# A two-layer recurrent block on one core: tiles by channel from memory, B's rows and the second layer's tokens turned through DRAM instead of on TensorE

## The reference

```
xn = layernorm(x)
# layer 0: RWKV-6 time mix (4 heads of 64) and a gated FFN with 2-of-4 sparsity
xx  = previous token of xn - xn
a   = tanh((xn + xx*maa_x) @ w1)            # five rank-32 mixes
x_f = xn + xx*(maa_f + a_f @ w2_f)          # f in w, k, v, r, g
y   = wkv6(r, k, v, w, u); out = groupnorm(y)*silu(g) @ W_o.T
ffn = sparsify_2to4(silu(xn@w_gate)*(xn@w_up)) @ w_down
# layer 1: state space layer (8 heads, state 64, head 64) and a gated FFN
inp, res = split(xn @ w_in.T); dt, B, C = split(xn @ w_param.T)
a   = exp(-softplus(dt))                    # decay of each head and token
S_t = a_t*S_(t-1) + B_t x_t^T ; y_t = C_t S_t
out = (y*silu(res)) @ w_out.T
```

## Time and profile before

| | |
|---|---|
| median of three runs | 761.48 us |
| the profiled execution | 761.46 us |
| its span | 759.7 us |
| busy: PE, DVE, ACT, POOL | 733.9, 505.5, 326.0, 76.6 us |

### The profile page before, as it was taken

How to read it: one execution, slowest core, us unless ns; L and a number is a source line. 1 busy time by engine, 2 the same in 40 slices (tenths; PEclk the granted TensorE clock), 3 DMA queues, 4 the chain that set the end, 5 groups by cost and what they waited for, 6 DMA issues and landing times.

```text
span 759.7 us, 18508 instructions
## 1 busy us (share of the span) xinstructions
PE 733.9 (97%) x7316; PEld 601.5 (79%) x7316; DVE 505.5 (67%) x1177; ACT 326.0 (43%) x659; POOL 76.6 (10%) x85
## 2 busy tenths in 40 slices
PE   5897999999999999999999999999999999999997
PEld 3775778877888788886888868888788878888686
DVE  3886578736797367955778467884679736796143
ACT  1322575226632466214752157512664236631570
POOL 6201011101011011000110001100011101101020
PEclk9999999999999999999999999999999999999999
DMA  8800410005000150002400032001500014000320
GB/s 284 330 16 0 127 30 3 1 30 154 2 3 1 48 135 2 3 2 71 113 2 2 3 126 57 3 1 30 149 8 2 1 45 140 2 3 1 99 55 16
DMA packets 33938, 39.77 MB, mean 52 GB/s; under 512 B 20352, under 2 KB 27968, under 8 KB 32192
## 3 DMA queue, kind: packets, MB, share of 16 engines
q1 hardware_dynamic: 33856, 38.49, 16.9%
HBM read 32.12 MB, written 6.36 MB: 51 GB/s over the span
## 4 chain that ended last, share of the span: by engine, by line
PE 93%; DVE 4%; issue 1%; ACT 1%; DMA 0%; POOL 0%; DVEq 0%; SPq 0%; ACTq 0%; POOLq 0%
PE psum L1276 70%; PE psum L1378 4%; PE psum L1488 2%; PE psum L1473 2%; PE psum L1338 2%; PE psum L1349 1%; PE psum L1499 1%; PE psum L1707 1%; PE psum L1526 1%; PE psum L1304 1%; PE psum L1324 1%; PE psum L1361 1%; PE psum L1434 1%; PE psum L1634 1%; PE psum L1441 1%
## 5 line engine op out<-in xcount | busy, mean ns | idle before, releaser
L519 ACT ACTIVATE BC<-psum 64x256 f32<-64x256 f32 x128 | 81.2, 634 | 3.5 <-PE psum L1276 1.8
L1276 PE MATMUL psum<-xnT,sb_f_gate 128*128 128x256 f32 x248 | 62.6, 396 | 1.0 <-ACT xnT L532 0.8
L1276 PE MATMUL psum<-xn1T,sb_n_gate 128*128 128x256 f32 x256 | 61.4, 383 | 0.0
L1276 PE MATMUL psum<-xn1T,sb_n_up 128*128 128x256 f32 x256 | 60.5, 379 | 0.0
L1276 PE MATMUL psum<-xnT,sb_f_up 128*128 128x256 f32 x240 | 58.3, 385 | 0.0
L1276 PEld LDWEIGHTS psum<-xnT,sb_f_gate 128*128 128x128 f32 x248 | 46.2, 194 | 9.9 <-issue 1.7
L1276 PEld LDWEIGHTS psum<-xn1T,sb_n_up 128*128 128x128 f32 x256 | 48.6, 190 | 6.6
L1276 PEld LDWEIGHTS psum<-xn1T,sb_n_gate 128*128 128x128 f32 x256 | 47.3, 190 | 6.5
L867 DVE TENSOR_TENSOR kT<-kT,dec 128x256 f32<-128x256 f32 x56 | 25.7, 458 | 36.0 <-PE psum L1378 29.0
L1276 PE MATMUL psum<-sb_n_down,hidB 128*128 128x256 f32 x224 | 49.5, 379 | 0.0
L1276 PE MATMUL psum<-sb_f_down,hid 128*128 128x256 f32 x224 | 49.5, 379 | 0.0
(11 more groups left out here) (209 smaller groups left out, 1517.1 us busy)
## 6 DMA issues: line engine op xcount, KB each, us to landing
cs_row<-cs_dram SPq DMA_DIRECT2D x8, 1024.0 KB, 5.5
x_dram<-gate SPq DMA_DIRECT2D x8, 512.0 KB, 2.8
cs_half<-cs_dram SPq DMA_DIRECT2D x16, 256.0 KB, 6.4
hidB<-x_dram SPq DMA_DIRECT2D x8, 512.0 KB, 8.1
X<-in_x SPq DMA_DIRECT2D x9, 256.0 KB, 2.7
x<-in_x SPq DMA_DIRECT2D x8, 256.0 KB, 4.1
out_tokens<-thFB SPq DMA_DIRECT2D x8, 256.0 KB, 2.2
sb_w_rkvgo<-in_w_rkvgo SPq DMA_DIRECT2D x1, 1280.0 KB, 5.9
```

What stands on the lines that cost most here:

```text
L519: ins = a_.activation(cols[:, par, 2 * pair:2 * pair + 2, :], src[64 * par:64 * par + 64, :, s, :], ACT.Identity)
L1276: ins = t_.matmul(ps(t, name)[first_row:first_row + rows, col:col + n], w, x, start=(k == 0), stop=(k == len(ws) - 1))
```

## The change

- x is given to the program a second time, by channel (`x_turned`). The next tile is loaded in both orders. Only the statistics come from the token order; mean and rstd go out to `row_dram` and come back on every partition (`token_rows`), and `next_normed` makes `xnT` directly. `next_turned` and its ScalarE copy are gone.
- B is turned in 32x32 blocks by two DVE instructions of 128x512 (`B_by_block`), stored in four transfers in pieces of 32 elements, and loaded as `Brow`; `B_decayed` scales `Brow` in place. `turned_B` is gone.
- The sums by position are read straight into `cs_pos`, one element at a time, instead of `cs16`; `turned_sums` is gone. `cs_row` has a semaphore of its own.
- The second layer's normed tokens are turned in 32x32 blocks on DVE, stored in eight transfers and loaded as `xn1T` (`channels_1`). Only the first tile is still turned by TensorE, now at the end of the first round.
- The first gate pair of the next tile is computed at the end of a round (`next_gate_0`, `next_up_0`) instead of at the head of the next.
- On DVE `end_args` and `B_by_block` go between level steps; the four counting operations of the sparsity go behind the level steps; the order of the decayed scores is 0, 2, hidden block 3, 1, 3. On ScalarE `end_exp` and `L_exps(0)` come before the tanh of res, `L_exps(1)` before `sums_exp`.
- The last combined round is written out instead of being in the loop.

```diff
-         ["xT1", "csum", "C1", "bt0", "sc1", "ys1", "n1u", "n3u"],
-         ["dt", "B0", "res0", "bt1", "sc3", "n0g", "n2g", "s1"],
+         ["csum", "C1", "sc1", "ys1", "n1u", "n3u"],
+         ["dt", "B0", "res0", "sc3", "n0g", "n2g", "s1"],
...
-            with eng.Fori(1, NT) as it:
+            with eng.Fori(1, NT - 1) as it:
                 one(Tile(it), Tile(it, -1))
+            one(Tile(None, NT - 1), Tile(None, NT - 2))
...
+            def token_rows(a):
+                wait(rstd_ready, a.count(3, 2))
+                wait(rows_loaded, a.count(16, 16))
+                sp_.dma_start(A["row_dram"].rearrange("(q p two) -> p q two", q=NQ, p=P),
+                              token_stats[:, :, :]).then_inc(rows_stored, 16)
+                wait(rows_stored, a.count(16, 16))
+                sp_.dma_start(rows[:, :, :].rearrange("p t two -> p (t two)"),
+                              A["row_dram"].partition_broadcast(P)).then_inc(rows_loaded, 16)
+
+            def channels_1(a, b):
+                wait(xn1_blocks, a.count(1, 0))
+                to = A["n_dram"].rearrange("(c j q g i) -> g q j c i", j=32, q=NQ, g=4, i=32)
+                blocks = xn1_turned[:, :].rearrange("p (c q i) -> p c q i", q=NQ, i=32)
+                for g_ in range(4):
+                    for q in range(NQ):
+                        sp_.dma_start(to[g_, q], blocks[32 * g_:32 * g_ + 32, :, q, :]).then_inc(xn1_stored, 16)
+                wait_filled(sp_, b, "n3u")
+                wait(xn1_stored, a.count(128, 16))
+                sp_.dma_start(xn1T[:, :, :], A["n_dram"].rearrange("(h p t) -> p h t", p=P, t=T)).then_inc(xn1_loaded, 16)
...
+                    sp_.dma_start(XT[:, :, :], channels(a.at() if last else a.next().at())).then_inc(xT_loaded, 16)
...
-                    sp_.dma_start(cs16[:, :], cs_dram.rearrange("(c p) -> c p", p=P)).then_inc(cs_loaded, 16)
-                    sp_.dma_start(flat(cs_row), cs_dram.partition_broadcast(P)).then_inc(cs_loaded, 16)
+                    sp_.dma_start(flat(cs_row), cs_dram.partition_broadcast(P)).then_inc(cs_rows_loaded, 16)
+                    sp_.dma_start(cs_pos[:, :], cs_dram.rearrange("(c p) -> p c", p=P),
+                                  allow_slow_non_contiguous=True).then_inc(cs_loaded, 16)
...
                     sp_.dma_start(Xrow.rearrange("p q c d -> p (q c) d"),
                                   x_dram.rearrange("(c p d) -> p c d", p=P, d=SD)).then_inc(X_rows, 16)
+                    if a:
+                        token_rows(a)
+                    wait(B_rows, b.count(16, 16))
+                    wait(B_blocks, b.count(2, 2))
+                    to = b_dram.rearrange("(s n i e d) -> s e i n d", s=NQ, i=32, e=2, d=32)
+                    for s in range(NQ):
+                        for e in range(2):
+                            r = 64 * s + 32 * e
+                            sp_.dma_start(to[s, e], B_turned[r:r + 32, :].rearrange("p (n d) -> p n d", d=32)).then_inc(
+                                B_stored, 16)
+                    wait(B_stored, b.count(64, 64))
+                    sp_.dma_start(Brow.rearrange("p q c d -> p (q c) d"),
+                                  b_dram.rearrange("(c p d) -> p c d", p=P, d=SD)).then_inc(B_rows, 16)
+                    if a:
+                        channels_1(a, b)
...
                 def next_normed():
-                    norm_apply(X, xn, a.count(3, 2), xn_ready)
-
-                    d.tensor_scalar(xnT[:, :, 0:1], xnT[:, :, T:T + 1], keep[:, bass.ds(a.next().at(), 1)], None,
-                                    ALU.mult).then_inc(carry_ready, 1)
+                    dve.wait_ge(rows_loaded, a.count(16, 32))
+                    dve.wait_ge(xT_loaded, a.count(16, 16))
+                    did(d.tensor_tensor(XT[:, :, :], XT[:, :, :], rows[:, :, 0].unsqueeze(1).to_broadcast([P, CH, T]),
+                                        ALU.subtract))
+                    did(d.tensor_scalar(xnT[:, :, 0:1], xnT[:, :, T:T + 1], keep[:, bass.ds(a.next().at(), 1)], None,
+                                        ALU.mult))
+                    after()
+                    d.tensor_tensor(xnT[:, :, 1:T + 1], XT[:, :, :], rows[:, :, 1].unsqueeze(1).to_broadcast([P, CH, T]),
+                                    ALU.mult).then_inc(xn_ready, 1)
...
+                    if b:
+                        dve.wait_ge(xn1_ready, a.count(1, 1))
+                        d.transpose(xn1_turned[:, :], flat(habs[:, 0:2, :])).then_inc(xn1_blocks, 1)
...
+                def B_by_block(half):
+                    wait_freed(dve, b, "B0")
+                    wait_freed(dve, b, "B1")
+                    n = slice(half * SEQ_T * SH // 2, (half + 1) * SEQ_T * SH // 2)
+                    d.transpose(B_turned[:, n], BC[:, 0, :, :].rearrange("p t h -> p (t h)")[:, n]).then_inc(B_blocks, 1)
...
                     level_step(a, 2)
+                    end_args()
+                    B_by_block(0)
+                    level_step(a, 3)
+                    B_by_block(1)
+                    level_step(a, 4)
                     sparse_compare(a, 0, 1)
                     sparse_compare(a, 0, 2)
-                    level_step(a, 3)
-                    sparse_sums()
-                    level_step(a, 4)
-                    sparse_rest()
                     level_step(a, 5)
...
-                        wait_freed(pe, b, "xT1")
+                        pe.wait_ge(xn1_loaded, b.count(16, 16))
...
-                    for s in range(NQ):
-                        wait_freed(pe, b, f"bt{s}")
+                    pe.wait_ge(B_ready, b.count(1, 1))
...
                 if a and b:
-                    gates_0()
-                    turned_1()
                     rank_mix()
...
-                    turned_sums()
-                    turned_B()
                     scores(0)
...
                     ffn_n(b, 3)
-                    next_turned()
                     out_1()
                     ffn_1(b, hidB)
+                    if a.reg is not None:
+                        next_gate_0()
+                        next_up_0()
```

More of the change, by code:

```diff
@@ L122, in build_block @@
         W = {n: sb("sb_" + n, list(A[n].shape)) for n in A
-             if n not in ("x", "out", "cs_dram", "x_dram", "w_mix2b", "w_dec2")}
+             if n not in ("x", "out", "x_turned", "n_dram", "row_dram", "cs_dram", "b_dram", "x_dram", "w_mix2b", "w_dec2")}
         W["w_mix2b"], W["w_dec2"] = sb("sb_mix2b", [NQ * DMIX, C]), sb("sb_dec2", [NQ * DDEC, C])
@@ L140, in build_block @@
         xn = sb("xn", [P, NQ, C])
+        XT = sb("XT", [P, CH, T])
+        token_stats = sb("token_stats", [P, NQ, 2])
+        rows = sb("rows", [P, T, 2])
         xnT = sb("xnT", [P, CH, T + 1])
@@ L187, in build_block @@
         cs_nat = sb("cs_nat", [P, NQ, SH])
-        cs16 = sb("cs16", [NQ * SCH, P])
+        cs_pos = sb("cs_pos", [P, NQ * SCH])
         cs_col = sb("cs_col", [P, NQ * SCH])
@@ L392, in one @@
                         out_stored, 16)
[L395 removed]
+            for s in (X_rows, X_stored, cs_stored, cs_loaded, cs_rows_loaded, B_rows, out_stored, rows_loaded, xn1_stored):
                 sp_.sem_inc(s, 16)
@@ L410, in _ @@
             load(["n_gate", "n_up", "n_down"], "ffn1")
+            token_rows(Tile(None, 0, first=True))
             with sp_.Fori(1, NT - 1) as it:
@@ L637, in out_scaled @@
                     free(ins, a, "yT")
-                def next_copied():
-                    act.wait_ge(carry_ready, a.count(1, 1))
-                    xnT_copy(a.next())
                 def ffn_tanh_1():
@@ L649, in one @@
                     ffn_tanh(a, "p0", th[0], th_ready)
-                    copy(b, xn1T[:, :, :], "xT1", CH)
                     rank_tanh()
@@ L715, in one @@
                     ffn_tanh_0()
-                    next_copied()
+                    copy(a, xn1T[:, :, :], "xT1", CH)
+                    wait_freed(act, a, "xT1")
+                    act.sem_inc(xn1_loaded, 16)
                 else:
-                    copy(b, xn1T[:, :, :], "xT1", CH)
                     x1_kept()
@@ L946, in differences @@
             def differences(t):
-                wait_freed(dve, t, "xT")
+                if t.first:
+                    wait_freed(dve, t, "xT")
+                else:
+                    dve.wait_ge(xn_ready, t.count(1, 1))
                 did(d.tensor_tensor(dxT[:, :, :], xnT[:, :, 0:T], xnT[:, :, 1:T + 1], ALU.subtract))
@@ L1160, in one @@
                     res_gate(1)
-                    end_args()
+                    sparse_count()
                     hidden_p(a, 2)
@@ L1542, in steps_turned, with next_gate_0, next_up_0 @@
                     close_bank(t_.transpose(ps(b, "dt")[:, 0:64], dtT, ident[64:P, 64:P]), b, "dt")
-                def gates_0():
-                    wait_freed(pe, a, "xT")
-                    ffn_p(a, 0)
+                def next_gate_0():
+                    pe.wait_ge(xn_ready, a.count(1, 2))
```

(7 more changed lines are left out.)

142 lines of the change are left out of this document (74 added, 68 removed).

## The result

The changed kernel takes 757.97 us (median of 17 runs, 755.71 to 761.2) against 761.24 (17 runs) before: ratio 0.9945, interval 0.9933 to 0.9958, so 0.55% faster, which is 4.2 us of 761.24 (the two medians themselves differ by 3.3 us). The forecast was 10.2 us. The profiled execution took 756.95 us with a span of 755.2 us; 749.5 was forecast. 5.7 us are missing.

What follows compares the result with a forecast made beforehand. TensorE, busy in 97% of the span, was taken to bound the kernel. 759.7 - 10.2 (removed turns) - 0.2 (first round) - 0.6 + 0.8 (last tile) = 749.5 us of span, 751.3 us with 1.8 more; range 748.5 to 763.

Steps and rivals of the forecast that it cites:

- the pitches of the removed turns: Seven combined rounds: TensorE loses 0.65 and 0.44 us in each, 0.43 in six of them, 10.2 us in all.
- Rival 4: The turns weren't the path and TensorE would wait elsewhere for DVE: 761.5 us; no change had chance 0.06.
- B's deadline: Middle rounds: B's rows land at about 389.5 us, 2.6 ahead of the deadline for DVE's scaling; cost 0.
- the sums by position: Loading cs_pos by single elements takes 2.6 us (bounds 1.2 to 7.7) against 8.3 of cover before end_args; costs nothing.
- the next norm: Next tile's norm: DVE pays +0.65 us where 1.3 us of short waits follow before the output projection; costs nothing.
- Rivals 2 and 3: B's rows come after 393.1 (775 us), or sums by position cost over 60 ns each (783 at 90); together 0.18.
- rival 1: A link of B's path takes part of the gain: priced 757 us; 0.26 together with rival 3's mild form.
- The moved gate pair only lengthens that idle time: End of the first round, before TensorE's turn: no cost, and the end comes 0.2 us earlier.
- It only changes what stands where: Gate pair moved from a round's head to the end of the round before: same 16 records, no price given.
- unrolling changes no instruction: nothing: Writing out the last combined round changes no instruction, so it was priced at nothing.
- The tokens' 0.6 us: Last tile: second-layer tokens arrive by memory at 706.6 instead of the copy's 707.74; -0.6 us, including 0.44 already counted.
- B's lateness: Last tile: B's stores stand behind the sums and X, scaling lasts to 738.0; net +0.8 us.

Runs made afterwards that it cites:

- e2: Changed kernel with 64 empty semaphore instructions ahead of TensorE's first work: 759.63 us, ratio 0.9952 to the kernel before.
- e3: Changed kernel with 160 empty semaphore instructions ahead of TensorE's first work: 772.47 us, ratio 1.0113 to the kernel before.
- e9: Changed kernel with first round reordered, counting early, B's stores before X in last tile, 64 empty instructions at three TensorE waits: 748.63 us, ratio 0.9827.
- e6: Changed kernel with B turned by TensorE again, no B through memory: 758.26 us, ratio 0.9931 to the kernel before.
- e11: Changed kernel with only the next tile's norm moved behind the centred chain in the first round: 758.78 us, ratio 0.9958.
- e12: Changed kernel with only the output product put ahead of the gate pair at the first round's end: 755.54 us, ratio 0.9916.
- e1: Changed kernel, first round only: next norm behind the centred chain, gate pair behind the output product: 755.22 us, ratio 0.9889 to the kernel before.
- e16: Changed kernel with e9's 64 empty instructions at the same three waits and no other edit: 756.70 us, ratio 0.9916.
- e14: Changed kernel with 32 empty semaphore instructions ahead of TensorE's first work: 770.21 us, ratio 1.0107 to the kernel before.
- e10: As e9 (first round, counting, last tile reordered) but without empty instructions: 752.79 us, ratio 0.9882 to the kernel before.
- e4: Changed kernel with cs_pos loaded contiguously in 64 B rows, output not the reference's: 760.45 us, ratio 0.9952 to the kernel before.
- e15: As e9 but with only the 32 empty instructions at the start: 761.54 us, ratio 0.9994 to the kernel before.

## Why the prediction failed

- **What bounds the kernel, and the pitches of the removed turns: right.** The middle periods without stops are 89.1 to 89.5 us in e2, e3 and e9 (89.1 by the sum), from 90.6. Rival 4 is out, and e6 shows the 14 turns of B at 0.55 us by themselves.
- **B's deadline, the sums by position, the second layer's tokens and the next norm, all in the middle rounds: right.** No TensorE group waits for a DMA there. Rivals 2 and 3 are out, and rival 1 is out in the middle rounds. That the time fell into rival 1's range (753.5 to 760, priced at 757) is luck: of its link through B only the last tile is there. One thing was missed: 0.16 us a round between scores and states, 0.11 of it from the counting operations.
- **"The moved gate pair only lengthens that idle time": the step that failed first.** The first round was priced -0.2 us and came out at +1.3, with 1.7 us of slow clock in the round behind it. The idle time was not free: after 3.20 us of it TensorE ran at 1.2 GHz, after 1.55 us it had not. The trace of the kernel before showed the low clock after its 3.04 us wait (0.63 in the window from 60 to 64), and the prediction gave no price to it. A second term was put at nothing there: the next tile's norm. Its +0.65 us on VectorE is covered in the middle rounds, but in the first round it stands ahead of the sparse half, and TensorE waits 3.78 us for that where it waited 3.04 (3.04 again in e11). e12 and e1 give these back (0.3 and 0.6%).
- **"It only changes what stands where", "unrolling changes no instruction: nothing": the second.** Both are true of the work and wrong for the time. TensorE's list got shorter and its last combined round was written out, so its code lay elsewhere, and 0.35 to 0.9 us of stops appeared in five of seven rounds, 2.3 us in all; the 2.0 us of four of them are what the next five rounds miss. Moving the code alone puts this kernel between 0.3% faster (e16, not clear of the noise) and 1.6% slower (e14) than it stands.
- **The last tile: one gain that was not there, one size off.** The tokens' 0.6 us were not gained, and not because of the load. The eight stores took 5.17 us to issue there (3.76 in a middle round), and TensorE waits 1.09 us for the load and then 0.39 for ScalarE. But in e9, where the load is in time, TensorE waits 1.55 us for ScalarE alone, one group later. The changed kernel, then e9:

```profile
702.16 0.63 PE L1600 MATMUL psum<-xn1T,sb_w_dt 128*32 128x128 f32 x8 [1.09 <-DMA xn1T<-n_dram]
...
705.10 0.24 PE L1627 MATMUL psum<-ident,aT_dtT 64*128 64x64 f32 x1 [0.39 <-ACT aT_dtT L620]
```

```profile
693.25 0.63 PE L1611 MATMUL psum<-xn1T,sb_w_dt 128*32 128x128 f32 x8
...
697.34 0.24 PE L1638 MATMUL psum<-ident,aT_dtT 64*128 64x64 f32 x1 [1.55 <-ACT aT_dtT L630]
```

  That copy stands on ScalarE behind the end of the tile before (`thFB` and `x_prev`). From ScalarE's `thFB` to this product it is 3.93 us in the kernel before, the changed kernel and e9 alike, so earlier tokens could bring nothing. B's lateness was forecast at +0.8 us net and measured +1.2, by the mechanism named: B's stores behind X.
- **Sum.** 1.5 + 1.1 + 0.3 in the first rounds, 2.0 in the middle, 0.9 at the end are the 5.7 us. With the order repaired the change gives 1.18% (e10), and with the code placed as well 1.73% (e9). Some 2.8 us of e9's gain come from a stop that the kernel before has too, and that kernel with 64 placed instructions was not run, so its 13.5 us are not all the change's. About the forecast's 10.2 us were there to be had, but not in the code as it lay.

That the stops move with the code's place and follow the transfers of instructions is shown; a rule for where they fall is not.

## What to carry to other kernels

In this kernel idle time of the bounding engine had a price beyond its length: look at the granted clock in the windows behind each wait of TensorE before a step is moved that lengthens it. Where a kernel is issue-dense and a change shortens or unrolls an engine's list, compare stops put down to "issue" first, and time one or two variants with empty instructions placed in an existing wait, before a difference under 1% is put down to the change. A removed instruction is worth its pitch in the steady rounds; the first and last rounds, where other waits end last, have to be priced by themselves.

## What the runs showed of the hardware

- Empty semaphore instructions on TensorE cost 0.15 us each while it has nothing else to do (14.7 us for 96, e2 to e3).
- A stop of 0.86 us in a stretch with other short waits is followed by 1.2 GHz (e10, clock 0.67 between 36 and 40; 1.00 in e9, which lacks the stop), as is one of 2.13 us (e14). The kernel before has the first (0.64). It does not always happen: the changed kernel's profiled execution has the same stop with the full clock behind it (1.00), and so does e6 with 1.8 us there.
- Stops of TensorE without a wait end 2.2 to 3.2 us after a 16 KB transfer of instructions started (62 of 62).
- Single elements of 4 B, 2048 of them, hold up the two issues behind them: 4.34 us against 1.09 (e4).
- Code that only moves costs a stop of up to 2.1 us a round at the loop's head in e14 and 2.2 in e15, and where the clock falls with it the round's first level comes 4.1 us late (e14).
